# Attention scores on one core: causal and window masks added by VectorE with the maxima, or by TensorE before them

## The reference

```
x = LN(x + windowed attention(x))      16 heads of 16, rotary, query i sees keys i-63 .. i
x = LN(x + channel mix(x))             sigmoid gate, squared relu, token shift
x = LN(x + linear attention(x))        64 random features
x = LN(x + block(x))                   causal attention (16 heads, rotary, all keys up to i), then 8 experts, top 2
```

```
attn = jnp.where(allowed, attn, -inf);  attn = softmax(attn)            # windowed
scores = jnp.where(causal, scores, -1e9);  probs = softmax(scores)      # causal
```

## Time and profile before

| | us |
|---|---|
| timed, median of 3 | 1938.33 (1937.84 to 1943.58) |
| the profiled execution | 1937.2 |
| its span, first to last instruction | 1935.3 |
| mean granted TensorE clock, share of full speed | 0.949 |

### The profile page before, as it was taken

How to read it: one execution, slowest core, us unless ns; L and a number is a source line. 1 busy time by engine, 2 the same in 40 slices (tenths; PEclk the granted TensorE clock), 3 DMA queues, 4 the chain that set the end, 5 groups by cost and what they waited for, 6 DMA issues and landing times. The chain is left out here.

```text
span 1935.3 us, 32833 instructions
## 1 busy us (share of the span) xinstructions
PE 1727.9 (89%) x10804; PEld 1102.1 (57%) x10804; DVE 1018.1 (53%) x2375; ACT 886.0 (46%) x1855; POOL 827.1 (43%) x1247
## 2 busy tenths in 40 slices
PE   4798998999999899999999999999269999999980
PEld 3565766565467556547755654555237776666750
DVE  2556677858566885847798677785201110001115
ACT  2354464557755364675546466766032222221212
POOL 4573664422377552237664233423533333334210
PEclk9898999999999899999999999999579999999995
DMA  5615235032444213244502214420323323333115
GB/s 186 88 24 66 34 79 67 13 56 67 58 68 92 29 18 50 67 66 68 104 9 34 34 47 66 68 67 2 110 88 81 83 40 72 76 85 84 22 19 179
DMA packets 93058, 124.17 MB, mean 64 GB/s; under 512 B 14064, under 2 KB 63152, under 8 KB 92736
## 3 DMA queue, kind: packets, MB, share of 16 engines
q1 hardware_dynamic: 78560, 105.24, 26.5%
q0 software_dynamic: 14336, 16.83, 5.3%
HBM read 45.70 MB, written 25.56 MB: 37 GB/s over the span
## 5 line engine op out<-in xcount | busy, mean ns | idle before, releaser
L1013 ACT ACTIVATE b_probs<-b_psum 128x512 f32<-128x512 f32 (+3 forms) x896 | 421.2, 538 | 212.0 <-PE b_psum L881 204.6
L1264 DVE TENSOR_REDUCE b_mneg<-b_psum 128x2 f32<-128x384 f32 (+5 forms) x608 | 335.2, 591 | 124.0 <-PE b_psum L868 121.9
L1359 POOL TENSOR_SCALAR_AFFINE_SELECT b_probs<-b_probs 128x512 f32<-128x512 f32 (+1 forms) x400 | 240.1, 612 | 330.3 <-ACT b_probs L1013 320.2
L868 PE MATMUL b_psum<-b_qk 96*128 96x192 bf16 (+4 forms) x1280 | 300.7, 299 | 2.2 <-DVE b_mhalf L1264 1.1
L881 PE MATMUL b_psum<-b_qk 99*128 99x192 bf16 (+5 forms) x1344 | 270.3, 290 | 13.6 <-DVE b_mneg L1264 4.8
L1645 DVE TENSOR_TENSOR b_ye<-b_psum,b_b2b 128x512 f32<-128x512 f32 x32 | 22.1, 692 | 428.2 <-PE b_psum L1600 428.2
L1624 ACT ACTIVATE b_hid<-b_psum,b_b 128x512 f32<-128x512 f32 x128 | 88.0, 687 | 317.3 <-PE b_psum L1591 317.3
L1553 POOL DMA_INDIRECT before_last_norm<-b_ye,b_ids x64 | 99.6, 1557 | 300.0 <-DMA before_last_norm<-b_ye,b_ids 159.9
L1600 PE MATMUL b_psum<-b_w,b_hid 128*128 128x256 f32 x1024 | 222.4, 379 | 0.8 <-ACT b_hid L1624 0.8
L1591 PE MATMUL b_psum<-b_xgt,b_w 128*128 128x512 f32 x512 | 221.2, 592 | 0.0
L1600 PEld LDWEIGHTS b_psum<-b_w,b_hid 128*128 128x128 f32 x1024 | 193.9, 190 | 27.6 <-ACT b_hid L1624 1.6
(11 more groups left out here) (212 smaller groups left out, 2444.2 us busy)
## 6 DMA issues: line engine op xcount, KB each, us to landing
b_qk<-b_split SPq DMA_DIRECT2D x372, 128.0 KB, 4.9
b_w<-in_W SPq DMA_DIRECT2D x16, 1024.0 KB, 7.8
b_src<-in_x SPq DMA_DIRECT2D x4, 1024.0 KB, 7.6
before_last_norm<-b_early SPq DMA_DIRECT2D x4, 1024.0 KB, 5.1
b_o<-before_last_norm SPq DMA_DIRECT2D x4, 1024.0 KB, 5.4
before_last_norm<-b_o SPq DMA_DIRECT2D x4, 1024.0 KB, 4.5
normed<-b_y SPq DMA_DIRECT2D x4, 1024.0 KB, 4.5
b_rows<-before_last_norm SPq DMA_DIRECT2D x8, 512.0 KB, 7.7
```

What stands on the lines that cost most here:

```text
L868: ins = pe.matmul(out[:, i, :], q[0:KS, h, P * t:P * t + P], q[0:KS, HG + h, a:e], start=not last, stop=True, skip_group_check=True)
L1013: act.activation(probs_of((g, h2, t), a, e)[:, heads[0]:heads[-1] + 1, :], bank, ACT.Exp, scale=SCALE).then_inc(s.exp_done, 1)
L1264: dve.tensor_reduce(out, in_bank(("max",) + x[1:], heads, e - a), AX.X, ALU.max, negate=True).then_inc(s.max_read, 1)
L1359: ins = pool.affine_select(out=block, in_=block, pattern=[[0, HG], [1 if ahead else -1, z - y]], compare_op=ALU.is_ge, fill=none, base=y - ...
```

## The change

`max` no longer writes a mask: each head's matmul starts its bank anew. `reduce` of a piece on the diagonal becomes one instruction for each head: it adds the bf16 mask (192 or 128 wide for windowed pieces; for causal ones the last columns of a 512-wide table, whose first 384 are zero) to the scores, writes the sum back to the same place in PSUM, and gives the maximum of the row. Since that instruction has no negation, the maxima are kept with their sign (b_mtop), `least` takes the larger, and the keys' rows hold -1.0 in place of 1.0. Unmasked pieces keep the one reduction. The planner's costs follow: no mask columns in `max`, 0.06 for each head in `reduce`. The table of masks loses its second copy.

```diff
@@ -53,6 +53,7 @@
 CT = CAP // P
 NEG = -2.0 ** 100
 EPS = 1e-5
+LOWEST = -3.0e38
 EARLY = 1
 BANK = 512
 DROPPED = 65536.0
@@ -365,8 +366,8 @@
                         n, w = len(x[0]), e - a
                         y = (("load", 0, 1, 2, t // 4) if g == 0 else ("load", g, 1, 2, None))
                         z = (("load", 0, 0, 5, t // 4) if g == 0 else ("load", g, 0, 5, None))
-                        add(("max", g, t, x), "PE", n * (0.003 + (w + (w if windowed[g] else P if mask else 0)) * 0.000417), y, z)
-                        add(("reduce", g, t, x), "DVE", 0.06 + n * w * 0.00104, ("max", g, t, x),
+                        add(("max", g, t, x), "PE", n * (0.003 + w * 0.000417), y, z)
+                        add(("reduce", g, t, x), "DVE", (0.06 * n if mask else 0.06) + n * w * 0.00104, ("max", g, t, x),
                             name("parts", g - 1, h))
             last = name("reduce", g, 4 * h + 3, self.pieces(g, *self.key_spans(g, 4 * h + 3)[-1])[-1])
             if h and not windowed[g]:
@@ -856,17 +857,9 @@
                     t, (heads, a, e) = x[2:]
                     load_done(pe, g, t // 4)
                     out = in_bank(x, heads, e - a)
-                    last = e == P * t + P
-                    if windowed[g]:
-                        pe.matmul(out, u.id16[:, :], u.mask_q[:, :, WQ - (e - a):WQ], start=True, stop=True,
-                                  skip_group_check=True)
-                    elif last:
-                        pe.matmul(out[:, :, P * t - a:P * t - a + P], u.id16[:, :],
-                                  u.causal_q[:, :].unsqueeze(1).broadcast_to([P, len(heads), P]), start=True, stop=True,
-                                  skip_group_check=True)
                     for i, h in enumerate(heads):
                         ins = pe.matmul(out[:, i, :], q[0:KS, h, P * t:P * t + P], q[0:KS, HG + h, a:e],
-                                        start=not last, stop=True, skip_group_check=True)
+                                        start=True, stop=True, skip_group_check=True)
                     ins.then_inc(s.max_ready, 1)
                 elif kind == "rows":
                     pe.wait_ge(s.m_parts, n + 1)
@@ -1258,15 +1251,22 @@
                     t, (heads, a, e) = x[2:]
                     dve.wait_ge(s.max_ready, n + 1)
                     some = slice(heads[0], heads[-1] + 1)
-                    out = u.mneg[:, some, t] if e == P * t + P else u.mhalf[:, some, t - 4]
+                    out = u.mtop[:, some, t] if e == P * t + P else u.mhalf[:, some, t - 4]
                     if g:
                         dve.wait_ge(s.m_parts, unit_number(g - 1, t // 4) + 1)
-                    dve.tensor_reduce(out, in_bank(("max",) + x[1:], heads, e - a), AX.X, ALU.max, negate=True
-                                      ).then_inc(s.max_read, 1)
+                    scores = in_bank(("max",) + x[1:], heads, e - a)
+                    if e == P * t + P:
+                        mask = u.mask_q[:, WQ - (e - a):WQ] if windowed[g] else u.causal_q[:, BANK - (e - a):BANK]
+                        for i, h in enumerate(heads):
+                            ins = dve.tensor_tensor_reduce(scores[:, i, :], scores[:, i, :], mask, 1.0, LOWEST, ALU.add, ALU.max,
+                                                           u.mtop[:, h, t:t + 1])
+                        ins.then_inc(s.max_read, 1)
+                    else:
+                        dve.tensor_reduce(out, scores, AX.X, ALU.max).then_inc(s.max_read, 1)
                 elif kind == "least":
                     dve.wait_ge(s.max_read, order[last_reduce(g, 1)] + 1)
-                    m = u.mneg[:, :, 4:8]
-                    dve.tensor_tensor(m, m, u.mhalf[:, :, :], ALU.min).then_inc(s.least_done, 1)
+                    m = u.mtop[:, :, 4:8]
+                    dve.tensor_tensor(m, m, u.mhalf[:, :, :], ALU.max).then_inc(s.least_done, 1)
                 elif kind == "divide":
                     h2 = x[2]
                     dve.wait_ge(s.out_ready, n + 1)
@@ -1300,7 +1300,7 @@
                     pool.wait_ge(s.least_done, order[("least", g, h)] + 1)
                 else:
                     pool.wait_ge(s.max_read, order[last_reduce(g, h)] + 1)
-                m = u.mneg[:, :, 4 * h:4 * h + 4]
+                m = u.mtop[:, :, 4 * h:4 * h + 4]
                 if n >= 2:
                     pool.wait_ge(s.rows_ready, n - 1)
                 parts = u.mparts[n % 2][:, 0:4 * 3 * HG].rearrange("p (t x) -> p t x", t=4)
@@ -1411,7 +1411,7 @@
         "c_id32": np.eye(P, dtype=np.float32),
 
         "c_tables": np.concatenate(
-            [np.eye(P), mask_q, mask_q, np.where(f <= p, 0.0, NEG),
+            [np.eye(P), mask_q, np.where(f <= p, 0.0, NEG),
              f >= p], 1).astype(np.float32),
         "c_blocks": (p // HD == f // HD).astype(np.float32),
         "c_iota": np.repeat(np.arange(E_, dtype=np.float32)[None], P, 0),
@@ -1429,14 +1429,14 @@
 def attention_buffers(nc, ctx, u):
     sbuf(nc, ctx, u, "cossin", [P, 2, NT, HG * HD])
     sbuf(nc, ctx, u, "id16", [P, P], BF16)
-    sbuf(nc, ctx, u, "mask_q", [P, 2, WQ], BF16)
-    sbuf(nc, ctx, u, "causal_q", [P, P], BF16)
+    sbuf(nc, ctx, u, "mask_q", [P, WQ], BF16)
+    sbuf(nc, ctx, u, "causal_q", [P, BANK], BF16)
     sbuf(nc, ctx, u, "src", [P, NT, D])
     sbuf(nc, ctx, u, "xt", [P, NC, T])
     sbuf(nc, ctx, u, "xa", [P, NC, T + 1])
     sbuf(nc, ctx, u, "o", [P, NT, D])
     sbuf(nc, ctx, u, "v", [P, 4, NT, HG * (HD + 1) + 15])
-    sbuf(nc, ctx, u, "mneg", [P, HG, NT])
+    sbuf(nc, ctx, u, "mtop", [P, HG, NT])
     sbuf(nc, ctx, u, "mhalf", [P, HG, NT - 4])
     sbuf(nc, ctx, u, "mrest", [P, 16])
     sbuf(nc, ctx, u, "ot_sb", [P, T])
@@ -1821,8 +1821,8 @@
     gram = ctx.enter_context(nc.semaphore("gram_ready"))
     names = "wqkv0 cossin id32 blocks iota next_token mur muk bq ln1g ln1b ln2g ln2b wgate".split()
     count = len(names) + 5 + P // HD
-    bf16_tables = (u.id16[:, :], u.mask_q[:, :, :], u.causal_q[:, :], u.upto[:, :])
-    width = [P, 2 * WQ, P, P]
+    bf16_tables = (u.id16[:, :], u.mask_q[:, :], u.causal_q[:, BANK - P:BANK], u.upto[:, :])
+    width = [P, WQ, P, P]
     tables = u.o[:, :, :].rearrange("p t d -> p (t d)")[:, 0:sum(width)]
     with nc.Block() as block:
         @block.sync
@@ -1850,13 +1850,14 @@
             dve.memset(u.one[:, :], 1.0)
             dve.memset(u.xa[:, :, 0:1], 0.0)
             dve.memset(u.minus[:, :], -1.0)
+            dve.memset(u.causal_q[:, 0:BANK - P], 0.0)
             for i in range(2):
                 dve.memset(u.mparts[i][:, :], 0.0)
             dve.memset(u.ones16[:, :], 1.0)
             dve.wait_ge(loaded, 16 * (count + 3))
             for i, t in enumerate(bf16_tables):
                 part = tables[:, sum(width[:i]):sum(width[:i + 1])]
-                dve.tensor_copy(t, part if width[i] == P else part.rearrange("p (h w) -> p h w", h=2))
+                dve.tensor_copy(t, part)
             dve.tensor_scalar(u.bk[:, :], u.bk[:, :], 1.0, None, ALU.add)
             dve.tensor_scalar(u.bq_plus[:, :], u.bq[:, :], 1.0, None, ALU.add).then_inc(fixed, 1)
             dve.wait_ge(gram, 1)
@@ -1865,7 +1866,7 @@
         @block.gpsimd
         def _(pool):
             for i in range(RING):
-                pool.memset(u.qk[i][KS:KS + 32, HG:2 * HG, :], 1.0)
+                pool.memset(u.qk[i][KS:KS + 32, HG:2 * HG, :], -1.0)
 
         @block.tensor
         def _(pe):
```

## The result

The changed kernel takes 1946.53 us (median of 10 runs, 1944.77 to 1948.1) against 1937.68 of the kernel before: ratio 1.004, 95% interval 1.0028 to 1.0052. Forecast was 1921 us, with 1886 to 1972 as the range: the time lies in it, the sign is wrong. The rival "VectorE paces the attention half" had the sign, not the size (1960 us). The rival "what TensorE saves it waits" is nearest in time (1938 us), though 8.5 us short.

A forecast was written before the change was run, and what follows sets the result against it. TensorE was taken as the bound of the attention half, VectorE second. From 1937.2 us, 66.6 saved on TensorE and 49.5 added through VectorE gave 1920.1, or 1921 us as the median of timed runs; range 1886 to 1972.

The forecast's parts named there:

- VectorE paces the attention half: Rival: longer rows of windowed pieces on VectorE make the kernel slower, middle about 1960 us; chance 0.34.
- what TensorE saves it waits: Rival: no change, TensorE waits in the attention half for what it saves, 1938 us; chance 0.16.
- The price is the distance of two starts: TensorE, attention half: removed mask columns priced at about 0.42 ns each by matmul start distances, 66.6 us saved.
- VectorE's price: Masked reductions on VectorE: 608 reductions become 1024 instructions, 165 us more likely, bounded by 50 and 248 us.
- The lower bound: The new VectorE call streams like a plain reduction, 119 ns fixed and 1.03 ns a column: 50 us more.
- my reason for leaving it: The call was likened to TENSOR_TENSOR from PSUM, plus a second small part of 72 ns writing the maximum: 165 us.
- The share that passes on: Attention half: 0.3 of VectorE's added 165 us reaches the end, 49.5 us, taken between 0.17 and a half.
- the planner, which I had said would soften little: Planner told only 0.06 us per extra VectorE instruction, 25 of the 165 us, so its order softens the loss little.
- nothing after 1313 us: The experts, some 620 us after the attention half, hold no mask or maximum and were carried over unchanged.
- a sign that TensorE starves: Sign of a wrong step: a lower granted clock in the attention half would mean TensorE is starved; no size given.
- the smaller edits: Fewer mask copies in the first DMA, a memset, the maxima's sign and two table copies: nothing together.
- the six shared PSUM banks: Attention half: VectorE was held to be the second bound behind TensorE, through these banks; no size given.

The follow-up runs named there:

- e1: Kernel before without its 608 mask matmuls, maxima taken over all keys of the span, planner order unchanged: 1918.92 us, ratio 0.9901.
- e2: Kernel before without any mask matmul, planner also told that the mask columns are gone, so another order: 1922.46 us, ratio 0.9916.
- e12: Kernel before without mask matmuls and with unmasked first-span reductions reading 256 of 512 columns, same order: 1902.55 us, ratio 0.9805.
- e11: Kernel before, its 256 unmasked first-span reductions reading 256 of 512 columns, masks kept, same order: 1924.1 us, ratio 0.9919.
- e3: Changed kernel with the planner's costs of the kernel before, so in that kernel's order and banks: 1960.08 us, ratio 1.0112.
- e10: Kernel before, planner told 0.119 us + 0.00103 a column for a reduction: 1922.54 us, ratio 0.9914.
- e9: Kernel before without mask matmuls, planner told of it and of 0.119 us + 0.00103 a column for a reduction: 1904.73 us, ratio 0.9831.

## Why the prediction was wrong

**The step that failed is the first: "The price is the distance of two starts", 66.6 us, put into the sum whole.** The distance of two starts is what a matmul takes from TensorE, and it was read correctly; it is not what the kernel gains. e1 shows 18.6 us for all of it (0.28), e2 15.0 in another order. I had put VectorE's added work through a share of 0.3 and TensorE's removed work through a share of 1, because TensorE was 95% busy in the stage rows. The test that I named there, a matmul starting when the columns of the one before have passed, was made on three matmuls of one row of pieces; the waits for maxima (51.6 us on weight loads of the two passes) and a clock that moves with the mask matmuls were not priced.

**VectorE's price**: 165 us forecast, 76.8 measured. The lower bound (119 ns and 1.03 ns a column) was right for the distance of two calls, and my reason for leaving it was half right. The result does cost an instruction of its own, dearer than I took it (141 ns, not 72), but in a row it runs beside the next call.

The two sentences on the Trainium skill, "VectorE: DVE Perf Modes", came out so. Its rule in the section "Two Vector instructions with no wait between them", that an accumulator output makes two instructions, agrees with this trace (1024 calls and 1024 reads). Its 120 fixed cycles for a source in PSUM, in the section on the TRN2 errata, are 125 ns and lie near the 119 ns that the starts show.

**The share that passes on**: 0.3 forecast. In one common order it is 0.47 to 0.54 (36.2 and 41.2 of 76.8 us). The changed kernel against e2, each in an order of its own (937 of their 2512 TensorE steps stand elsewhere), is 24.1 us slower, 0.31 of 76.8. That this is my 0.3 is luck: the planner, which I had said would soften little, gave 13.6 us back.

**The sum, taken apart**: -15.0 (e2) + 24.1 (the changed kernel against e2) = +9.1 us, against the +8.9 of the result. The two steps lead from one kernel to the other, so they must add up; this says where the time is and tests nothing. The forecast's terms were -66.6 + 49.5 = -17.1. It took the gain 51.6 us too large and the loss 25.4 us too large, and the second error hid half of the first: with the right price of VectorE at the share of 0.3 it would have been further off (-66.6 + 23.0).

**What held**: nothing after 1313 us changed by more than 1.1 us; no mask matmul is left; VectorE stays under 90% in the attention half (971 of 1271 us up to 1316.9, 76%); the granted clock fell, which the prediction had named as a sign that TensorE starves. Of the rivals, "what TensorE saves it waits" named what e1 shows for a part of the saving. No run takes the smaller edits by themselves.

**Open**: why the causal masks add almost nothing to the gain (1.6 of 27.3 us), when a relief of VectorE does not free them (e12 against e11: 21.5 us for all masks, 18.6 without the relief). And how the lost 44.7 us divide by cause: the account gives 16.1 to the clock and leaves 28.6, beside which the waits for maxima grew by 22.9. That the six shared PSUM banks carry the coupling of the two engines, as the prediction has it, is argued: no run changed their number.

## What to carry to other kernels

Put removed work through a share as well as added work: in a fixed order an engine that is 95% busy gave back a quarter of what was taken from it; the rest stands in this account as a lower clock and as more waiting. Price an instruction with an accumulator by the distance of starts in a row, never by adding the two means. Before shifting work between engines, ask whether the result needs it at all: a softmax's subtracted maximum may include masked keys, and leaving the masks out of that pass was worth 1% where moving them cost 0.4%. With a masked key far above the allowed ones the exponentials of the whole row can vanish; how large a distance is safe was not measured here.

## What the hardware showed that I had not expected

- The read of VectorE's accumulator (141 ns, 1024 of them) starts with the next call (both at 100.07 us) and adds nothing in a row, where the fixed part stays at the 119 ns of a plain reduction.
- A call that adds and takes the maximum, in place in PSUM with a bf16 mask from SBUF, runs at 1.03 ns a column, the pace of a plain reduction, which only reads.
- The granted TensorE clock followed the mask matmuls: 0.946 to 0.950 with them in the kernel before, 0.937 to 0.940 (e1) and 0.933 to 0.936 (e3) without, and with half the first spans 0.948 to 0.953 with them (e11) and 0.938 to 0.946 without (e12), all in the same order, at nearly the same share of busy time (87 to 89%). It is no rule for masks: with the planner's measured costs it is 0.952 to 0.958 with them (e10) and 0.943 to 0.952 without (e9), so the order of the work moves it by as much.
